# Delta attention with compact 32-token blocks and 32x32 tile products, given tile by tile

## The chip, the cores and the metric

One core of one Trainium2 chip runs the whole program in one launch. The metric is the device time of an execution in microseconds. The kernel computes four transformer layers in nine stages, one after the other with a barrier between them; the change touches the second stage, `delta_attention`, alone.

## The reference, cut to what matters

The stage computes layer 0's attention, for 2 sequences of 1024 tokens and 16 heads of 128 keys and 128 values. For each head and token a key `k`, a query `q`, a value `v`, a vector of decays `exp(g)` and a scalar `beta` come from projections and a short convolution; then

```python
def step(S, inp):
    q_t, k_t, v_t, g_t, b_t = inp
    S = S * jnp.exp(g_t)[..., None]
    kv = jnp.einsum('bhk,bhkv->bhv', k_t, S)
    delta = (v_t - kv) * b_t[..., None]
    S = S + k_t[..., None] * delta[..., None, :]
    o_t = jnp.einsum('bhk,bhkv->bhv', q_t * scale, S)
    return (S, o_t)
```

All numbers are fp32.

## The kernel before, in words

**Units and slots.** The work is cut into `NU0` = 64 units, each one head and one group of 512 tokens (`GRP`), that is four chunks (`NC`) of 128 tokens (`P`). A loop over slots `g` on each engine issues a fixed order of pieces; a unit starts every `SL` = 7 slots, and each piece of it has its slot (`K_AT`, `VT_AT`, ..., `LV_AT` = 17, `CHUNK_AT` = 24, `Y_AT` = 31), so the pieces of about five units lie beside each other in one slot. Every engine works its list in order; semaphores tie them, and a wait stops everything behind it on that engine. The order on each engine is written by hand, in the blocks `pe` (line 287), `act` (486), `pool` (597) and `dve` (674). Weights come by DMA per head on the SP queue (line 284).

**Levels.** Within a chunk the recurrence is unrolled into a triangular system. Its matrix, and the matrix from keys to outputs, are built in seven levels `lv` = 0 to 6 of doubling block size `h` = 2^lv, one level per slot. `products` (294) multiplies keys `kF` with the odd half-blocks of scaled keys and queries `kq`: per chunk one matmul with 128 columns of weights and 128 moving columns into the bank `lpd`. `mask` (689) on VectorE copies those entries that belong to the level (`pairs`) into `MA[:, lv]` (the system) and `MA[:, LV + u % 2]` (the output matrix). `scale` (606) on GpSimd multiplies the decays of the level into `kq` and `kF`. The first level's transpose is taken on TensorE (464).

**The inverse.** `Tm` holds the transposed inverse of the system built so far and `TT` the inverse, each 512 columns wide, a full 128x128 block per chunk. Each level from 1 to 6 updates them: X = `MA` times the even half-blocks of `Tm` (389), copied to `Xs` by ScalarE (555); Y = `TT` times X (434; 436 at level 6), subtracted from `Tm` by VectorE (829; 769 at level 6); `transposed` (302) turns `Tm` and ScalarE copies the odd half-blocks into `TT` (517). All this shares the bank `xy`.

**The chunks.** With the inverse, a unit's four chunks go one per slot through the state `St`: W = `kq` times `St` (372), `R` on VectorE (759), delta = `TT` times `R` (408), copied to `Dl` (552), then the state's update (449), and the outputs from the state (445) and from `MA`'s output matrix (450). Line 366 computes the diagonal of the output matrix, multiplied by the identity on VectorE (825). `VT`, `STAT`, `Z`, `KH`, `SUMS`, `OUT`, `Y` and `GATE` are the unit's other pieces: transposes of values, norms, decays, keys, the normalised and gated output and its projection (401).

**Array tiles.** A matmul may name a part of the 128x128 array by `tile_position` (first row, first column). Before the change only line 331 does so in this stage (weights of 32 columns); the last attention stage has 64-row and 64-column ones (1925, 1939, 1944). Line 436 has weights of 64 columns. An fp32 matmul appears in the trace as two MATMUL records and two LDWEIGHTS records, a transpose as one of each.

## Time and profile before

| what | value |
|---|---|
| median of 2 runs | 6401.66 us (6400.4 to 6402.93) |
| the profiled execution's own time | 6396.97 us |
| its span | 6394.8 us, 99261 instructions |
| TensorE busy | 5965.5 us, 93% |
| VectorE busy | 3804.0 us, 59% |
| ScalarE busy | 2694.1 us, 42% |
| GpSimd busy | 2288.9 us, 36% |

PE is TensorE's matmuls, PEld its weight loads, which run beside them; DVE is VectorE, ACT ScalarE, POOL GpSimd, SP the engine that issues DMAs. A busy share averages over nine stages with different limits, so the stage's own stretch is what counts. In a group's row, "128*64 128x64" is the used part of the array (rows*columns of weights) and the moving operand; after the bar stand busy time, the mean length of one record, and the engine's idle time just before the group with what ended it. Matmuls are pipelined: a record lasts longer than the step from one start to the next.

### The profile page before, as it was taken

What the parts mean: (1) busy time and instruction counts of PE and PEld (TensorE: products, weight loads), DVE (VectorE), ACT (ScalarE), POOL (GpSimd) and SP (SyncE); (2) the same over time, 40 slices, a digit from 0 to 9 for tenths busy, and PEclk for the clock granted to TensorE, in tenths of its full rate; (3) what the DMA queues carried; (4) which work ended last, traced back from release to release, by engine and by line L of the source; (5) the groups of instructions that cost most, each with busy time, mean ns of one, the idle gap of its engine ahead of it and who ended that gap; (6) DMA issues with size and microseconds to landing.
All of it is one profiled execution on the core that took longest, in us unless ns stands there. A gap on an engine that the chain in (4) does not pass through costs nothing. (4 is left out here: it accounts for less than half of the span.)

```text
span 6394.8 us, 99261 instructions
## 1 busy us (share of the span) xinstructions
PE 5965.5 (93%) x37522; PEld 4271.9 (67%) x37522; DVE 3804.0 (59%) x7226; ACT 2694.1 (42%) x5584; POOL 2288.9 (36%) x2602
## 2 busy tenths in 40 slices
PE   5999999999999999997999999989999999999999
PEld 3777777777777777775677777643335667766665
DVE  6778787787877878773344444266634444444322
ACT  4554555545555455541355555215662122222221
POOL 4677777777777777772000000020000011111100
PEclk8999999999999999998999999989999999999999
DMA  0000000000000000000000000000001011121200
GB/s 30 5 5 5 5 5 1 5 5 5 5 5 5 5 5 5 1 1 15 15 11 13 14 11 9 20 7 1 1 1 53 18 64 64 64 70 64 71 7 7
DMA packets 33926, 112.56 MB, mean 18 GB/s; under 512 B 4273, under 2 KB 9649, under 8 KB 33457
## 3 DMA queue, kind: packets, MB, share of 16 engines
q1 hardware_dynamic: 33456, 106.22, 4.9%
q8 instruction: 305, 5.00, 0.3%
q14 instruction: 165, 1.34, 0.1%
HBM read 104.11 MB, written 2.10 MB: 17 GB/s over the span
## 5 line engine op out<-in xcount | busy, mean ns | idle before, releaser
L616 POOL TENSOR_TENSOR d_kq<-d_kq,d_tot 128x512 f32<-128x512 f32 x448 | 543.0, 1212 | 742.2 <-PE d_lpd L299 731.3
L683 DVE SCALAR_TENSOR_TENSOR d_qkv<-d_raw,d_wts,d_qkv 128x512 f32<-128x512 f32 x576 | 531.9, 924 | 43.1 <-ACT d_qkv L492 35.6
L299 PE MATMUL d_lpd<-d_kq,d_kF 128*128 128x128 f32 x3584 | 520.5, 290 | 33.9 <-POOL d_kq L646 27.2
L299 PEld LDWEIGHTS d_lpd<-d_kq,d_kF 128*128 128x128 f32 x3584 | 458.9, 199 | 58.0 <-POOL d_kq L646 26.7
L389 PEld LDWEIGHTS d_xy<-d_Tm,d_MA 128*128 128x128 f32 x3072 | 388.6, 196 | 92.3 <-issue 90.8
L389 PE MATMUL d_xy<-d_Tm,d_MA 128*128 128x64 f32 x3072 | 406.1, 276 | 43.9 <-ACT d_TT L517 43.9
L694 DVE COPY_PREDICATED d_MA<-d_pairs,d_lpd 128x512 f32<-128x512 int32 x384 | 317.6, 827 | 134.2 <-PE d_lpd L299 123.4
L1001 POOL TENSOR_TENSOR f1rstd<-f1var,mhalf 128x4 f32<-128x4 f32 x4 | 4.0, 1009 | 1090.1 <-DVE f1var L1026 1090.1
L1787 DVE TENSOR_REDUCE r_nm<-r_ps 128x2 f32<-128x1024 f32 x256 | 307.8, 1222 | 142.4 <-PE r_ps L1606 142.3
L290 PE MATMUL d_fr<-xnT,d_wts 128*128 128x512 f32 x768 | 367.1, 601 | 5.3 <-DMA d_wts<-in_headw 5.3
L1885 PE MATMUL e_pj<-xnT,e_wts 128*128 128x512 f32 x768 | 348.1, 603 | 14.3 <-DMA e_wts<-in_w3all 12.3
L617 POOL TENSOR_TENSOR d_kF<-d_kF,d_tot 128x256 f32<-128x256 f32 x448 | 342.4, 764 | 0.0
L1707 ACT ACTIVATE r_pT<-r_ps 128x512 f32<-128x512 f32 x512 | 275.0, 598 | 148.5 <-PE r_ps L1614 147.9
L434 PE MATMUL d_xy<-d_Xs,d_TT 128*128 128x64 f32 x2560 | 329.5, 273 | 0.0
L697 DVE SCALAR_TENSOR_TENSOR d_lp<-d_lp,d_ez 128x512 f32<-128x512 f32 x448 | 310.9, 694 | 13.2
L434 PEld LDWEIGHTS d_xy<-d_Xs,d_TT 128*128 128x128 f32 x2560 | 318.6, 196 | 0.0
L1238 PEld LDWEIGHTS c_po<-c_pT,c_vt 128*128 128x128 f32 x2304 | 294.7, 191 | 20.8 <-ACT c_pT L1303 9.0
L1341 DVE TENSOR_TENSOR c_sc<-c_sc,c_mask 128x128 f32<-128x128 f32 x256 | 76.7, 300 | 382.5 <-PE c_sc L1193 382.3
L1238 PE MATMUL c_po<-c_pT,c_vt 128*128 128x128 f32 x2304 | 301.8, 276 | 0.2
L1606 PE MATMUL r_ps<-r_kT,r_qT 32*128 32x512 f32 x1024 | 294.1, 697 | 3.1 <-DVE r_nm L1787 1.6
L1193 PE MATMUL c_sc<-c_kT,c_qT 128*128 128x512 f32 (+3 forms) x768 | 290.2, 487 | 0.7 <-ACT c_qT L1264 0.7
L1614 PE MATMUL r_ps<-r_qT,r_kT 32*128 32x512 f32 x1024 | 279.5, 652 | 0.8 <-ACT r_pT L1707 0.8
...
## 6 DMA issues: line engine op xcount, KB each, us to landing
...
```

Of the source, the lines that this page charges most:

```text
L290: last = nc.tensor.matmul(fr[:, bank, :], w_of(u)[:, w0 + kd * P:w0 + (kd + 1) * P], T.xnT[:, kd, tok(u):tok(u) + GRP], start=(kd == 0), s ...
L299: last = nc.tensor.matmul(out[:, :, k], kF[:, u % 2, ch_(k)], moving[:, :, k, :, 1], start=True, stop=True)
L389: last = nc.tensor.matmul(mh(xy[:, j * 64:(j + 1) * 64], h), MA[:, lv, ch_(j)], even(Tm[:, ch_(j)], h), start=True, stop=True)
L434: last = nc.tensor.matmul(xy[:, 256 + j * 64:256 + (j + 1) * 64], TT[:, ul % 2, ch_(j)], Xs[:, j * 64:(j + 1) * 64], start=True, stop=True)
L616: nc.gpsimd.tensor_tensor(v, v, bc(bc(t_l[:, :, 0], 2, h), 1, 2), ALU.mult)
L617: nc.gpsimd.tensor_tensor(f, f, bc(t_l[:, :, 1], 2, h), ALU.mult)
L683: step = nc.vector.scalar_tensor_tensor(qkv[:, u % 3, x], raw[:, u % 2, x, i:i + GRP], tap(u, x, i), qkv[:, u % 3, x], ALU.mult, ALU.add)
L694: nc.vector.copy_predicated(into, bc(mh(pairs[:, lv], h), 1, 2), lpd[:].rearrange("p (x m h) -> p x m h", x=2, h=h)).then_inc(masked, 1)
L697: ch.link(nc.vector.scalar_tensor_tensor(lp[:], lp[:], LOG1P[i], ez[:], ALU.add, ALU.mult))
L1238: last = nc.tensor.matmul(po[:, 0:P], vt[:, n // (4 * QT) % 2, j], pT[:, n % 2, j * P:(j + 1) * P], start=(j == 0), stop=(j == t))
L1787: nc.vector.tensor_reduce(nm[:, t % 2, half, 4 * j + i0:4 * j + i0 + 2], ps[:, row_pair(row - 1):row_pair(row - 1) + 2], AX, ALU.max).then ...
L1885: last = nc.tensor.matmul(pj[:, x % 2, :], w[:, w0 + kd * P:w0 + (kd + 1) * P], T.xnT[:, kd, g * GRP:(g + 1) * GRP], start=(kd == 0), stop ...
```

## The change

The system is first built and inverted in compact blocks of 32 tokens: for levels 0 to 4 a matrix is kept as four bands of 32 partitions (`NB` = 4, `BW` = 32) with 32 columns for each chunk, 128 columns in all instead of 512 (`MB` for the masked products, `TB` for the inverse and its transpose). `products` below level `BL` = 5 gives, for each of four column tiles of the array, four chunks with 32 columns of weights and 32 moving columns. `in_blocks` gives 32x32 products, blocks outside and chunks inside. In levels 1 to 4 both Y and its transpose are computed as products (`Tb(0)`, `Xb` in either order), so that `transposed` and the copies into `TT` go. At level 5 ScalarE spreads the compact blocks into `TT` and `Tm` (six copies), at level 4 those of the output matrix into `MA` (four copies); level 5 works on pairs of blocks, level 6 on 64x64 tiles. A small identity `eye` is loaded besides. The wide products of levels 5 and 6, GpSimd's `scale`, the chunks and all other pieces are unchanged.

```diff
+BL = 5
+BW = 1 << BL
+NB = P // BW
...
-        MA = sb("MA", [P, LV + 2, GRP])
-        Tm, TT, Xs = sb("Tm", [P, GRP]), sb("TT", [P, 2, GRP]), sb("Xs", [P, GRP // 2])
+        MA, MB = sb("MA", [P, LV - BL + 2, GRP]), sb("MB", [P, BL + 2, P])
+        TB, TT, Tm = sb("TB", [P, 2, P]), sb("TT", [P, 2, GRP]), sb("Tm", [P, GRP // 2])
+        Xs = sb("Xs", [P, GRP // 2])
...
                 def products(u, lv):
                     h = 1 << lv
-                    out = lpd[:].rearrange("p (x c m h) -> p x c m h", x=2, c=NC, h=h)
-                    moving = kq[:, u % 2].rearrange("p x (c m two h) -> p x c m two h", c=NC, two=2, h=h)
-                    for k in range(NC):
-                        last = nc.tensor.matmul(out[:, :, k], kF[:, u % 2, ch_(k)], moving[:, :, k, :, 1], start=True, stop=True)
+                    if lv < BL:
+                        out = lpd[:, 0:P].rearrange("p (x c m h) -> p x c m h", x=2, c=NC, h=h)
+                        moving = kq[:, u % 2].rearrange("p x (c r m two h) -> p x c r m two h", c=NC, r=NB, two=2, h=h)
+                        for r in range(NB):
+                            for k in range(NC):
+                                last = nc.tensor.matmul(out[band(r), :, k], kF[:, u % 2, blk(k, r)], moving[:, :, k, r, :, 1], start=True, stop=True,
+                                                        tile_position=(0, BW * r), skip_group_check=True)
+                    else:
+                        out = lpd[:].rearrange("p (x c m h) -> p x c m h", x=2, c=NC, h=h)
+                        moving = kq[:, u % 2].rearrange("p x (c m two h) -> p x c m two h", c=NC, two=2, h=h)
+                        for k in range(NC):
+                            last = nc.tensor.matmul(out[:, :, k], kF[:, u % 2, ch_(k)], moving[:, :, k, :, 1], start=True, stop=True)
                     last.then_inc(p_mm, 1)
 
-                def transposed(u):
-                    for k in range(NC):
-                        last = nc.tensor.transpose(xy[:, ch_(k)], Tm[:, ch_(k)], T.ident[:])
-                    last.then_inc(tr_mm, 1)
+                def in_blocks(at_col, left, right, blocks, shift_in, shift_out):
+                    for r in blocks:
+                        for k in range(NC):
+                            i, o = band(r + shift_in), band(r + shift_out)
+                            last = nc.tensor.matmul(xy[o, at_col + k * BW:at_col + (k + 1) * BW], left(i, k, r), right(i, k, r), start=True, stop=True,
+                                                    tile_position=(i.start, o.start), skip_group_check=True)
+                    return last
+
+                Tb = lambda x: lambda i, k, r: TB[i, x, k * BW:(k + 1) * BW]
+                Xb = lambda i, k, r: Xs[i, k * BW:(k + 1) * BW]
+                eye_b = lambda i, k, r: eye[i, :]
+                low_b = lambda lv: lambda i, k, r: MB[i, lv, k * BW:(k + 1) * BW]
+                next_b = lambda i, k, r: MA[i, 0, blk(k, r + 1)]
...
-                        for j in range(NC):
-                            last = nc.tensor.matmul(fr[:, 2, ch_(j)], kF[:, u % 2, ch_(j)], qkv[:, u % 3, 0, ch_(j)], start=True, stop=True)
+                        for r in range(NB):
+                            for j in range(NC):
+                                last = nc.tensor.matmul(fr[band(r), 2, j * BW:(j + 1) * BW], kF[:, u % 2, blk(j, r)], qkv[:, u % 3, 0, blk(j, r)],
+                                                        start=True, stop=True, tile_position=(0, BW * r), skip_group_check=True)
...
+                        elif lv < 6:
+                            pe.wait_ge(tb_ready, 4 * ul + lv - 1)
                         else:
-                            pe.wait_ge(tm_ready, 5 * ul + lv - 1)
-                            pe.wait_ge(tt_ready, 5 * ul + lv - 1)
-                        h = 1 << lv
-                        for j in range(NC):
-                            last = nc.tensor.matmul(mh(xy[:, j * 64:(j + 1) * 64], h), MA[:, lv, ch_(j)], even(Tm[:, ch_(j)], h), start=True, stop=True)
+                            pe.wait_ge(t5_ready, ul + 1)
+                            pe.wait_ge(t_spread, ul + 1)
+                        if lv < 5:
+                            last = in_blocks(0, low_b(lv), Tb(1), range(NB), 0, 0)
+                        elif lv == 5:
+                            last = in_blocks(0, next_b, Tb(1), (0, 2), 0, 1)
+                        else:
+                            for j in range(NC):
+                                last = nc.tensor.matmul(xy[64:, j * 64:(j + 1) * 64], MA[0:64, 1, j * P + 64:(j + 1) * P], Tm[0:64, j * 64:(j + 1) * 64],
+                                                        start=True, stop=True, tile_position=(0, 64), skip_group_check=True)
...
                         pe.wait_ge(xs_ready, 6 * ul + lv)
-                        for j in range(NC):
-                            if lv < 6:
-                                last = nc.tensor.matmul(xy[:, 256 + j * 64:256 + (j + 1) * 64], TT[:, ul % 2, ch_(j)], Xs[:, j * 64:(j + 1) * 64], start=True, stop=True)
-                            else:
-                                last = nc.tensor.matmul(xy[0:64, 256 + j * 64:256 + (j + 1) * 64], Xs[:, j * 64:(j + 1) * 64], odd(TT[:, ul % 2, ch_(j)], 64)[:, 0],
-                                                        start=True, stop=True)
+                        if lv < 5:
+                            in_blocks(P, Xb, Tb(0), range(NB), 0, 0)
+                            last = in_blocks(2 * P, Tb(0), Xb, range(NB), 0, 0)
+                        elif lv == 5:
+                            in_blocks(P, Xb, Tb(0), (0, 2), 1, 0)
+                            last = in_blocks(2 * P, Tb(0), Xb, (0,), 1, 1)
+                        else:
+                            for j in range(NC):
+                                last = nc.tensor.matmul(xy[0:64, 256 + j * 64:256 + (j + 1) * 64], Xs[64:, j * 64:(j + 1) * 64],
...
-                        last = nc.tensor.matmul(co[:, ch_(k)], Dl[:, ch_(k)], MA[:, LV + uc % 2, ch_(k)], start=fresh, stop=True)
+                        if k == 0:
+                            pe.wait_ge(out_spread, uc + 1)
...
                         pe.wait_ge(mask0_ready, ul + 1)
-                        for j in range(NC):
-                            last = nc.tensor.transpose(xy[:, ch_(j)], MA[:, 0, ch_(j)], T.ident[:])
-                        last.then_inc(tr_mm, 1)
...
-                    if level and 1 <= lv < 6:
-                        pe.wait_ge(tm_ready, 5 * ul + lv)
-                        transposed(ul)
 
...
-                    if level and lv >= 2:
-                        act.wait_ge(tr_mm, 6 * ul + lv)
-                        h = 1 << lv - 1
-                        nc.scalar.activation(odd(TT[:, ul % 2], h), odd(xy[:], h), ACT.Copy).then_inc(tt_ready, 1)
+                    if level and lv == 5:
+                        act.wait_ge(tb_ready, 4 * ul + 4)
+                        for r in range(NB):
+                            nc.scalar.activation(TT[band(r), ul % 2].rearrange("p (c r i) -> p c r i", c=NC, r=NB)[:, :, r], c3(TB[band(r), 0]), ACT.Copy)
+                        for r in range(2):
+                            last = nc.scalar.activation(Tm[band(r)].rearrange("p (c r i) -> p c r i", c=NC, r=2)[:, :, r], c3(TB[band(r), 1]), ACT.Copy)
+                        last.then_inc(t_spread, 1)
+                    if level and lv == 4:
+                        act.wait_ge(masked, 7 * ul + 5)
+                        for r in range(NB):
+                            last = nc.scalar.activation(MA[band(r), 2 + ul % 2].rearrange("p (c r i) -> p c r i", c=NC, r=NB)[:, :, r], c3(MB[band(r), BL + ul % 2]), ACT.Copy)
+                        last.then_inc(out_spread, 1)
...
-                        nc.scalar.activation(Xs[:], xy[:, 0:256], ACT.Copy).then_inc(xs_ready, 1)
+                        rows, cols = (slice(64, P), 256) if lv == 6 else (slice(0, P), P)
+                        nc.scalar.activation(Xs[rows, 0:cols], xy[rows, 0:cols], ACT.Copy).then_inc(xs_ready, 1)
...
-                nc.gpsimd.memset(MA[:, 0:LV], 0.0).then_inc(consts_set, 1)
-                pool.wait_ge(consts_set, 4)
+                for t in (MA, MB, TT, Tm):
+                    nc.gpsimd.memset(t[:], 0.0).then_inc(consts_set, 1)
...
                 def mask(u, lv):
                     h = 1 << lv
-                    gap = LV + u % 2 - lv
-                    into = MA[:, lv:lv + gap + 1:gap].rearrange("p x (m two h) -> p x m two h", two=2, h=h)[:, :, :, 1]
+                    t, a, o, n = (MB, lv, BL, 64) if lv < BL else (MA, lv - BL, 2, 256)
+                    gap = o + u % 2 - a
+                    into = t[:, a:a + gap + 1:gap].rearrange("p x (m two h) -> p x m two h", two=2, h=h)[:, :, :, 1]
                     dve.wait_ge(p_mm, 7 * u + lv + 1)
-                    nc.vector.copy_predicated(into, bc(mh(pairs[:, lv], h), 1, 2), lpd[:].rearrange("p (x m h) -> p x m h", x=2, h=h)).then_inc(masked, 1)
+                    if lv == BL:
+                        dve.wait_ge(out_spread, u + 1)
+                    nc.vector.copy_predicated(into, bc(mh(level_pairs(lv), h), 1, 2), lpd[:, 0:2 * n].rearrange("p (x m h) -> p x m h", x=2, h=h)).then_inc(masked, 1)
 
...
-                        t = odd(TT[0:64, ul % 2], 64)
-                        nc.vector.tensor_tensor(t, t, mh(xy[0:64, 256:512], 64), ALU.subtract).then_inc(tt6_ready, 1)
+                        nc.vector.tensor_scalar(odd(TT[0:64, ul % 2], 64), mh(xy[0:64, 256:512], 64), -1.0, None, ALU.mult).then_inc(tt6_ready, 1)
...
+                        if ul:
+                            dve.wait_ge(t_spread, ul)
+                        nc.vector.tensor_tensor(c3(TB[:, 0]), bc(eye[:], 1, NC), c3(MB[:, 0]), ALU.subtract).then_inc(tt0_ready, 1)
...
-                        nc.vector.tensor_tensor(c3(Tm[:]), bc(T.ident[:], 1, NC), c3(xy[:]), ALU.subtract).then_inc(tm0_ready, 1)
+                        dve.wait_ge(tr_mm, ul + 1)
+                        nc.vector.tensor_tensor(c3(TB[:, 1]), bc(eye[:], 1, NC), c3(xy[:, 0:P]), ALU.subtract).then_inc(tm0_ready, 1)
...
                         dve.wait_ge(dg_mm, u + 1)
-                        nc.vector.tensor_tensor(c3(MA[:, LV + u % 2]), c3(fr[:, 2, :]), bc(T.ident[:], 1, NC), ALU.mult).then_inc(diag_ready, 1)
+                        if u >= 2:
+                            dve.wait_ge(out_spread, u - 1)
+                        nc.vector.tensor_tensor(c3(MB[:, BL + u % 2]), c3(fr[:, 2, 0:P]), bc(eye[:], 1, NC), ALU.mult).then_inc(diag_ready, 1)
                     if level and 1 <= lv < 6:
                         dve.wait_ge(yt_mm, 6 * ul + lv)
-                        h = 1 << lv
-                        nc.vector.tensor_tensor(even(Tm[:], h), even(Tm[:], h), mh(xy[:, 256:512], h), ALU.subtract).then_inc(tm_ready, 1)
+                        if lv < 5:
+                            nc.vector.tensor_tensor(TB[:], TB[:], xy[:, P:3 * P].rearrange("p (x i) -> p x i", x=2), ALU.subtract).then_inc(tb_ready, 1)
+                        else:
+                            for r in (0, 2):
+                                nc.vector.tensor_scalar(TT[band(r), ul % 2].rearrange("p (c r i) -> p c r i", c=NC, r=NB)[:, :, r + 1], c3(xy[band(r), P:2 * P]),
+                                                        -1.0, None, ALU.mult)
+                            nc.vector.tensor_scalar(Tm[band(1)].rearrange("p (c r i) -> p c r i", c=NC, r=2)[:, :, 0], c3(xy[band(1), 2 * P:3 * P]),
+                                                    -1.0, None, ALU.mult).then_inc(t5_ready, 1)
                     if chunk:
...
-    f["pairs"] = np.ascontiguousarray(np.stack([np.tile((j2 >> l) == 2 * (m2 >> l), (1, 4)) for l in range(LV)], 1).astype(np.int32))
+    low = [np.tile(((j2 % BW) >> l) == 2 * (m2[:, :BW // 2] >> l), (1, NC)) for l in range(BL)]
+    high = [np.tile((j2 >> l) == 2 * (m2 >> l), (1, NC)) for l in range(BL, LV)]
+    f["pairs"] = np.concatenate(low + high, 1).astype(np.int32)
```

## Rows read from the trace of the kernel before

**Rows 1.** The page, section 1: busy us (share of the span) x instructions.

```profile
PE 5965.5 (93%) x37522; PEld 4271.9 (67%) x37522; DVE 3804.0 (59%) x7226; ACT 2694.1 (42%) x5584; POOL 2288.9 (36%) x2602
```

**Rows 2.** Busy us by stretch: length, PE, PEld, DVE, ACT, POOL; clock, DMA, GB/s.

```profile
24.00:2940.00 2916.00, 2639.03 (x18415) 2125.31 (x18414) 2278.74 (x4441) 1454.69 (x2960) 2052.97 (x2382) 0.98 0.02 5
1504.00:1548.00 44.00, 40.95 (x294) 32.79 (x292) 35.12 (x70) 22.71 (x47) 32.04 (x37) 1.00 0.00 1
5361.12:5364.12 3.00, 3.00 (x49) 2.67 (x48) 2.31 (x4) 0.00 (x0) 0.00 (x0) 1.00 0.74 261
```

**Rows 3.** Line 346 alone: ns min/median/max, first and last start.

```profile
L346 PE MATMUL d_fr<-d_qkv,d_wsv x128: 592/595/1062, 53.0 to 2824.5; 128*128 128x512 f32 x128
```

**Rows 4.** TensorE's groups, 200 to 2600 us: busy, mean ns, idle before, releaser.

```profile
L299 PE MATMUL d_lpd<-d_kq,d_kF 128*128 128x128 f32 x3032 | 437.0, 288 | 20.1 <-POOL d_kq L646 18.1
L389 PE MATMUL d_xy<-d_Tm,d_MA 128*128 128x64 f32 x2600 | 340.7, 275 | 34.4 <-ACT d_TT L517 34.4
...
L304 PE MATMUL d_xy<-ident,d_Tm 128*128 128x128 f32 x1080 | 168.0, 278 | 9.7 <-DVE d_Tm L829 9.7
L401 PE MATMUL d_fr<-d_wo,d_og 128*128 128x256 f32 x432 | 107.7, 392 | 15.6 <-DVE d_MA L825 15.6
...
L408 PE MATMUL d_ca<-d_R,d_TT 128*128 128x128 f32 x434 | 96.0, 303 | 12.0 <-DVE d_R L759 11.9
L449 PE MATMUL d_ca<-d_Dl,d_khat 128*128 128x128 f32 x432 | 87.4, 284 | 66.1 <-ACT d_Dl L552 66.1
...
L372 PE MATMUL d_ca<-d_St,d_kq 128*128 128x128 f32 x382 | 82.9, 299 | 35.0 <-DVE d_St L835 21.7 <-DVE d_St L833 13.3
```

**Rows 5.** TensorE's timeline, around 1502 us: start us, us, instructions merged.

```profile
1502.11 1.00 PE L389 MATMUL d_xy<-d_Tm,d_MA 128*128 128x64 f32 x8
...
1503.23 1.06 PE L299 MATMUL d_lpd<-d_kq,d_kF 128*128 128x128 f32 x8
1504.12 1.02 PE L434 MATMUL d_xy<-d_Xs,d_TT 128*128 128x64 f32 x8
...
1505.70 0.61 PE L304 MATMUL d_xy<-ident,d_Tm 128*128 128x128 f32 x4
```

**Rows 6.** TensorE's timeline in the last attention stage, 5361 us.

```profile
5361.12 1.16 PE L1925 MATMUL e_md<-e_qkT 64*128 64x128 f32 x16
5362.22 1.09 PE L1939 MATMUL e_po<-e_at,e_v 128*64 128x128 f32 x16
5363.24 0.44 PE L1944 MATMUL e_po<-e_qdT,e_carry 64*64 64x128 f32 x4
5363.51 0.82 PE L1944 MATMUL e_po<-e_qdT,e_mid 64*64 64x128 f32 x12
5364.26 1.16 PE L1952 MATMUL e_md<-e_v,e_kvd 128*128 128x128 f32 x8
5365.26 0.69 PE L1885 MATMUL e_pj<-xnT,e_wts 128*128 128x512 f32 x1
```

**Rows 7.** Line 436's form, and narrow windows of the timeline (436, then 331).

```profile
L436 PE MATMUL d_xy<-d_TT,d_Xs x512: 222/222/366, 147.6 to 2933.8; 128*64 128x64 f32 x171
...
1522.71 0.40 PE L436 MATMUL d_xy<-d_TT,d_Xs 128*64 128x64 f32 x4
...
1499.12 0.64 PE L331 MATMUL d_fr<-d_sqs,d_pick 128*32 128x512 f32 x4
```

**Rows 8.** Copies and masks of VectorE and ScalarE, 200 to 2600 us.

```profile
L694 DVE COPY_PREDICATED d_MA<-d_pairs,d_lpd 128x512 f32<-128x512 int32 x326 | 270.1, 828 | 98.1 <-PE d_lpd L299 88.3
...
L517 ACT ACTIVATE d_TT<-d_xy 128x256 f32<-128x256 f32 x270 | 104.9, 389 | 149.9 <-PE d_xy L304 149.8
...
L552 ACT ACTIVATE d_Dl<-d_ca 128x128 f32<-128x128 f32 x217 | 60.9, 281 | 306.9 <-PE d_ca L408 306.9
```

**Rows 9.** Timeline of the stage's start, GpSimd and TensorE.

```profile
28.83 3.08 POOL L603 MEMSET d_MA<- 128x3584 f32 x1
...
32.46 8.06 PE L290 MATMUL d_fr<-xnT,d_wts 128*128 128x512 f32 x12 [5.34 <-DMA d_wts<-in_headw]
```

32 lines of the change are left out of this document (20 added, 12 removed).

## The prediction

> **What bounds the kernel now.** I read the page's busy shares first, then the busy time by stretch, then one projection's first and last start to get the rhythm, then the matmul groups with what they waited for, and the timeline last, to price one record. Of the span TensorE is busy 93% [rows 1]. The delta attention stage lasts from about 24 to 2940 us; inside it TensorE is busy 2639 of 2916 us, VectorE 2279, GpSimd 2053, ScalarE 1455 [rows 2]. Line 346 runs once per unit (one head and 512 tokens, 64 units): (2824.5 - 53.0) / 63 = 43.99 us per unit [rows 3]. In one such period TensorE works 40.95 us, VectorE 35.12, GpSimd 32.04, ScalarE 22.71 [rows 2]. So TensorE sets the pace, and what is left are waits: the seven groups of [rows 4] idle 192.9 us in 2400 us, or 54.6 units, 3.5 us per unit: 1.2 for `Dl` (L449), 0.64 for `St` (L372), 0.63 for the `TT` copy (L389), 0.37 for `kq` (L299), 0.29 for the diagonal (L401), 0.22 for `R` (L408), 0.18 for `Tm` (L304). VectorE and GpSimd have 9 and 12 us of air.
>
> **What one record costs.** An fp32 matmul leaves two records, each with its weight load; a transpose leaves one. Less the last one's own length, 0.288 us, eight products of L299 take (1.06 - 0.29) / 7 = 0.11 us a record [rows 4, 5]. L389 and L434 stream only 64 columns and cost the same (1.00 and 1.02 us for eight) [rows 5]: the 128 columns of weights set the step. A transpose takes (0.61 - 0.28) / 3 = 0.11 us. With 64 columns of weights the step is (0.40 - 0.222) / 3 = 0.059 us [rows 7]. Records on *different* tiles start together: four 512-column ones, 0.59 us each, lie within 0.64 us [rows 7], and sixteen on two tiles take 1.16 us where eight on the full array take 1.16 [rows 6].
>
> **The change, part by part, per unit.**
>
> *Counts.* Now the touched groups hold 56 (products) + 8 (diagonal) + 48 (X) + 48 (Y) + 24 (transposes) = 184 records, the rest 104, together 288; the trace has 294 in 44 us [rows 2]. After: nineteen sets of sixteen 32-wide matmuls (products of levels 0 to 4, the diagonal, four X, eight in four Y, the transposing one) are 608 records; level 5 has 16 + 24, level 6 has 8 + 8, the wide products of levels 5 and 6 have 16: 680, and 784 with the rest.
>
> *Array time.* The order is tile outside, chunk inside, so four successive matmuls share a tile and cannot lie on top of each other; only at three tile borders in a set can two start together. From 0.112 and 0.059 us at 128 and 64 columns, 53 ns per 64 columns, 32 columns give 0.032 us. No row shows 32 by 32; the bounds are 0.030 (half of 0.059) and 0.059 (nothing more to gain). I take 0.032, since the two rows lie on a line with their columns. A set costs 32 x 0.032 less the borders, 0.9 us, exactly what the wide group of eight costs (8 x 0.112). Now: 19 wide groups x 0.9 + 24 transposes x 0.11 + level 6's Y 0.46 = 20.2 us. After: 19 x 0.9 + level 5 0.5 + 0.7 + level 6 2 x 0.46 + two wide products 1.8 = 21.0 us. **+0.8 us.** A quarter of the area per matmul is paid back by four times as many of them.
>
> *Changing the array's shape.* From L1925 (64 rows) to L1939 (64 columns) and on to L1944 (64x64) and L1952 (full) the next group starts 0.20 us after the start of the last record before it (a group's end less the 0.27 to 0.29 us that a record lasts, [rows 4]), instead of 0.11 as from L1952 to L1885, where the shape stays [rows 6]. That is 0.09 us of draining, and then the first weights load uncovered: 0.03 us for 32 columns, 0.10 for 128. So 0.12 us into a narrow shape, 0.19 back. In program order of the new code the shape changes 33 times per unit (five times in each of the slots of levels 0, 1, 2, 3 and 6, four in those of 4 and 5), against 2 now (L436): 18 more into narrow shapes, 13 more into the full one: 18 x 0.12 + 13 x 0.19 = **+4.6 us.** Bounds: 0, if every drain falls into a wait, and 6 with 0.19 for all.
>
> *Waits removed.* The 20 transposes of `Tm` and the `TT` copies go, with 0.63 + 0.18 us of waits. More TensorE work stands between the first `St` and its use, and between scalings and products: of 0.64 + 0.37 + 0.22 us I take 1.1 as covered. `Dl` and the diagonal keep theirs. **-1.9 us** (bounds -2.0 and -0.8).
>
> *Waits added.* ScalarE gets four copies at level 4 and six at level 5, of 32 partitions x 128, for five `TT` copies of 0.389; the nearest row is 0.281 for 128x128 [rows 8]. Behind the level 4 copies stand the `stat` copy and `Xs`, behind those of level 5 `Xs`; the products between X and Y (0.9 us plus two shape changes) and the `stat` transposes cover most. **+0.3 us** (bounds 0 and 0.9: ten copies at 0.281 less five at 0.389, all exposed). VectorE's four masks shrink from 0.828 us [rows 8] and three of its 512-column subtractions too: priced at nothing, because it is not the bound; if TensorE's excess vanished that would count. `copy_predicated` of `out` at level 5 waits for a spread that was issued a slot earlier: nothing. GpSimd's scalings do not change. At the start its memsets grow from 3584 to 4224 columns, 3.08 to 3.6 us, ending near 32.5 us, while TensorE projects from 32.46 for 8 us before it needs them [rows 9]; the small identity's DMA lands in the same time.
>
> *Sum.* 0.8 + 4.6 - 1.9 + 0.3 = +3.8 us per unit, a period of 47.8; x 64 = +243 us. The profiled execution took 6396.97 us (span 6394.8), 5 us below the median of 6401.66, so 6640 either way.
>
> **Rivals.**
> *Tiles overlap in spite of the order* (faster). If loads and matmuls of the next tile passed those of the tile at work, four tiles would run at once, as L331's four do, and 648 narrow records would take a quarter: 15 us less. TensorE would fall to about 30 us and GpSimd's 32 and the level chain would bind; I put the period at 38: 6397 - 6 x 64 = 6010. It decides as soon as more than 4 us are overlapped. Against it: in L1925 to L1944 records start in pairs and never more, as the tiles alternate [rows 6]. The Trainium skill, TensorEngine Tiling (Array Packing), sections Theoretical Speedup and Key Properties, says that different tiles load and multiply in parallel and gives 4x for one dimension of 32; by that alone this rival would be the forecast. The rows grant it to neighbours in program order only. 0.12.
> *Drains are hidden* (no change): if changes of shape mostly fall where TensorE waits anyway, or the two narrow shapes need none, 1 to 2 us of the 4.6 remain: 6400 to 6530. For it: 3.5 us of waits; against: they sit at few places (L449, L372), the changes at all. 0.16.
> *Records have a floor.* If 32 columns still cost 0.059, 648 x 0.027 = +17.5 us: 6397 + 21.3 x 64 = 7760. The straight line through two rows speaks against. 0.12.
> *Supply.* The densest stretch is 49 records in 3.00 us, 0.061 each [rows 2]; if no more can be sustained, 784 x 0.061 = 47.8 plus the 1.2 us wait for `Dl`, 49.0: 6717. 0.10. The Trainium skill, TensorE: Matmul & The Clock Gate, section Wait — 56ns, not 53.3ns?, has about 62 ns per matmul for a sequencer that decodes in software; no run here shows in which mode this chip is, and by it the sum would be 784 x 0.062 + 1.2 = 49.8 us, about 6770.
>
> **Numbers.** The forecast (6530 to 6800) has 0.50. Likeliest time 6640. Two per cent, what a measurement of this kernel tells from no change, is 128 us: 6274 to 6530. Faster 0.12, same 0.15, slower 0.73. The range leaves out the faster rival and the full floor: 6440 (drains mostly hidden) to 7150 (a price of about 0.045 us, halfway between the bounds: 13 ns x 648 = 8.4 us more per unit, 6640 + 540).
>
> **What would show it.** Period of L346 near 47.8 us. A set of sixteen narrow matmuls spans 0.9 + 0.2 us from first start to last end: at 0.3 the overlap rival holds, at 1.7 the floor. Between groups of different shape the next start comes 0.20 us after the last. TensorE busy rises above 93%, VectorE's share falls, no wait for `TT` or `Tm` is left, and the `Dl` wait stays at about 1.2 us. I am wrong if the narrow records do not stand one behind another, or if waits for `Xs` or `TB` of over 1 us per unit appear on TensorE.

## Result: 2.96% slower, near the predicted time, by another route

The changed kernel takes 6587.59 us (median of two runs, 6582.71 to 6592.48) against 6401.66 before: a ratio of 1.0296, 95% interval 1.0277 to 1.0316. The forecast was 6640 within 6440 to 7150. The profiled execution of after spans 6590.7 us, 195.9 more than before's 6394.8, and all of it is in the delta attention stage: the projection that marks the unit (L346 before, L372 now) runs from 53.3 to 3016.6 us, a period of (3016.6 - 53.3) / 63 = **47.04 us** against 43.99 [rows 3], and 3.05 x 64 = 195 us.

The profile after, first its busy shares and TensorE's granted clock in 40 slices, then the clock row of before:

```profile
PE 6158.9 (93%) x69266; PEld 4298.0 (65%) x69266; DVE 3610.1 (55%) x7354; ACT 2755.4 (42%) x5904; POOL 2273.2 (34%) x2605
...
PEclk8898999899888989998899999999999999999999
...
PEclk8999999999999999998999999989999999999999
```

The share of TensorE is the same 93% as before [rows 1]. The stage is the first 19 slices, and of these 9 read 8 in the clock row; of before, 1 of the first 18 does. The stretches that answer to [rows 2], with one unit cut in four (us, then busy time of PE, PEld, DVE, ACT, POOL, then the clock):

```profile
24.00:3130.00 3106.00, 2826.17 (x50154) 2148.49 (x50152) 2085.69 (x4568) 1513.61 (x3277) 2035.97 (x2383) 0.90 0.02 6
1504.00:1551.00 47.00, 41.95 (x782) 32.60 (x782) 32.07 (x71) 23.64 (x51) 31.79 (x37) 0.93 0.01 3
1504.00:1526.00 22.00, 20.80 (x376) 15.79 (x374) 17.17 (x38) 10.65 (x26) 13.18 (x16) 1.00 0.01 2
1526.00:1533.00 7.00, 4.63 (x47) 3.76 (x45) 4.86 (x9) 1.84 (x5) 6.76 (x6) 0.78 0.01 4
1533.00:1541.00 8.00, 6.51 (x108) 4.70 (x107) 4.68 (x13) 4.62 (x8) 5.18 (x7) 0.76 0.01 3
1541.00:1551.00 10.00, 10.00 (x258) 8.35 (x260) 5.36 (x15) 6.53 (x14) 6.66 (x10) 1.00 0.01 3
```

The count of 782 records is the predicted 784. The clock was 0.98 in the stage before [rows 2] and is 0.90 now, and in this unit all of the loss lies between 1526 and 1541 us. TensorE's groups from 200 to 2600 us, to be read beside [rows 4]; that is 2400 / 47.04 = 51.0 units, where before has 54.6:

```profile
L299 PE MATMUL d_fr<-xnT,d_wts 128*128 128x512 f32 x600 | 341.8, 699 | 0.0
L310 PE MATMUL d_lpd<-d_kq,d_kF 128*32 128x32 f32 x8128 | 248.0, 206 | 71.8 <-POOL d_kq L692 70.4
L323 PE MATMUL d_xy<-d_TB,d_Xs 32*32 32x32 f32 x7264 | 217.7, 197 | 7.0 <-ACT d_Xs L600 6.9
...
L436 PE MATMUL d_fr<-d_wo,d_og 128*128 128x256 f32 x408 | 145.9, 521 | 9.7 <-DVE d_MB L877 9.7
...
L443 PE MATMUL d_ca<-d_R,d_TT 128*128 128x128 f32 x408 | 99.0, 326 | 2.6 <-DVE d_R L808 2.2
...
L488 PE MATMUL d_ca<-d_Dl,d_khat 128*128 128x128 f32 x406 | 83.7, 288 | 77.9 <-ACT d_Dl L596 77.9
...
L423 PE MATMUL d_xy<-d_Tm,d_MA 64*64 64x64 f32 x400 | 35.1, 231 | 16.6 <-DVE d_MA L743 16.6
```

The waits for `TT`, `Tm` and `St` are gone and that for `R` is 0.05 us per unit. But TensorE waits 71.8 / 51 = 1.41 us per unit for `kq0` (0.37 before), 1.53 for `Dl` (1.21) and 0.33 for the level 6 mask. And an untouched line has become slow: the Y projection, L436, takes 521 ns a record; the same work was 392 (L401 in [rows 4]).

**Where the period went.** For every pair of successive TensorE records of the same two lines I took the mean step from start to start in stretches at the full clock, and multiplied by how often the pair occurs. That is the unit's work at the full clock. What the same steps took beyond it I call clock cost; idle time is the rest. In us per unit, from the traces between 200 and 2600 us:

```
                          period  full-clock work  clock cost  waits
before                     43.99      39.87          0.58      3.52
after                      47.04      39.49          3.92      3.62
chunks outside             43.70      32.07          4.87      6.75
chunks outside + fill      43.05      34.78          3.32      4.95
after + fill at the waits  45.24      42.16          1.71      1.35
after + fill elsewhere     49.10      41.85          3.95      3.29
before + fill              44.98      41.72          0.47      2.79
before + six narrow        45.97      41.31          0.98      3.68
before + six wide          45.03      41.02          0.50      3.52
kq0 first                  50.58      42.46          4.95      3.15
kq0 first + fill           45.74      42.28          1.62      1.86
moved work, chunks outside 43.65      32.80          3.07      7.78
moved work + fill, same    44.99      34.41          2.77      7.80
before + moved work        44.84      39.00          1.55      4.28
```

(Some pairs never ran at the full clock, so their steps count as work: 8 us per unit in the row of kq0 first, 1.1 to 1.3 in the rows of moved work on the chunk order, 0.2 or less in the others. There the work is overstated and the clock cost is at least what stands in the row.) So the +3.05 us of the change are **-0.4 of work, +3.3 of clock, +0.1 of waits**. I had +5.4, 0 and -1.6. The traces' clock records add up to 68 us at the lower level (1.2 GHz) in these 2400 us before and 447 after. (Some expectations below carry such sums taken from a stretch 11 us earlier, up to 8 us larger.)

**Why kq0 is late.** GpSimd's timeline of the same unit:

```profile
1516.21 3.97 POOL L681 TENSOR_TENSOR d_pw<-d_st,d_half 128x20 f32<-128x20 f32 x1 [0.61 <-DVE d_sums L760]
...
1521.34 1.05 POOL L662 TENSOR_TENSOR d_kq<-d_kq,d_tot 128x512 f32<-128x512 f32 x1
...
1523.07 1.01 POOL L704 TENSOR_TENSOR d_rr<-d_ms,mhalf 128x4 f32<-128x4 f32 x1
...
1524.59 1.08 POOL L678 TENSOR_TENSOR d_hid<-d_pw,d_mlp 128x256 f32<-128x256 f32 x1
1525.64 1.05 POOL L685 TENSOR_TENSOR d_hid<-d_sums,d_mlp 128x256 f32<-128x256 f32 x1
1526.77 1.81 POOL L692 TENSOR_TENSOR d_kq<-d_qkv,d_tot 128x512 f32<-128x512 f32 x1
```

From the power of the sums to `kq0` it is one serial row of work, 10.6 us from 1516.21 to 1526.77, and it was as long before (10.7, 1511.87 to 1522.55). In the mean of the units between 200 and 2600 us the wait grows by 1.07 us. Counted from the `stat` transposes, TensorE arrives at the products of level 0 only 0.24 us earlier than before (13.79 us against 14.03), and `kq0` ends 1.0 us later, so that the products start 0.83 later. Of the 1.0, 0.59 is the start of the row (2.80 us after the `stat` transposes against 2.21): it needs the sums (L500, L459 before), and ahead of these now stand two sets of narrow products for Y instead of one wide group. The row itself is 0.21 longer, and `kq0` takes 1.68 us instead of 1.48. TensorE's timeline behind it:

```profile
1528.63 0.90 PE L310 MATMUL d_lpd<-d_kq,d_kF 128*32 128x32 f32 x32 [2.37 <-POOL d_kq L692]
1529.46 3.31 PE L436 MATMUL d_fr<-d_wo,d_og 128*128 128x256 f32 x8
...
1534.69 0.46 PE L488 MATMUL d_ca<-d_Dl,d_khat 128*128 128x128 f32 x2 [1.49 <-ACT d_Dl L596]
...
1537.04 2.08 PE L519 MATMUL d_fr<-d_g1T,d_wts 128*128 128x512 f32 x2
```

L436 takes 3.31 us; the same work took 1.99 at the full clock before (L401, at 1525.02 us). L519 takes 2.08, and took 1.02 (L480, at 1531.03). In this unit the clock falls behind the waits, at 1530.0 and 1536.8 us, and what pays is wide work that the change never touched. Over all units it is not so simple. Between 200 and 2600 us the clock falls 99 times. In the 14 us before 65 of these falls TensorE stood idle for 0.2 us or more in all, and they bring 283 us at the lower level. In those before the other 34 it did not, and they bring 164 us; these lie at one place of the unit, 18 to 24 us after the first record of L372, a stretch with narrow groups throughout. (The stretch of 14 us is my choice; 7 and 10 us give the same counts.) Before the change all 20 falls follow idle time. That the clock falls *because* of the waits was a guess here; the experiments below bear it out for the first kind.

### The profile page after: what moved, and what is told of

The parts are those of the page before. It is cut to its first block and busy times, and to the rows that moved or that the text cites. A ratio compares the mean times of both kernels' runs of the same rounds, so it can differ in the third digit from the quotient of the medians.

```text
span 6590.7 us, 163265 instructions
## 1 busy us (share of the span) xinstructions
PE 6158.9 (93%) x69266; PEld 4298.0 (65%) x69266; DVE 3610.1 (55%) x7354; ACT 2755.4 (42%) x5904; POOL 2273.2 (34%) x2605
## 5 line engine op out<-in xcount | busy, mean ns | idle before, releaser
L729 DVE SCALAR_TENSOR_TENSOR d_qkv<-d_raw,d_wts,d_qkv 128x512 f32<-128x512 f32 x576 | 551.8, 958 | 47.7 <-ACT d_qkv L528 45.1
L299 PE MATMUL d_fr<-xnT,d_wts 128*128 128x512 f32 x768 | 435.4, 697 | 5.4 <-DMA d_wts<-in_headw 5.4
L310 PE MATMUL d_lpd<-d_kq,d_kF 128*32 128x32 f32 x10240 | 313.7, 206 | 101.3 <-POOL d_kq L692 94.9
L310 PEld LDWEIGHTS d_lpd<-d_kq,d_kF 128*32 128x32 f32 x10240 | 276.6, 119 | 141.4 <-POOL d_kq L692 97.0
L596 ACT ACTIVATE d_Dl<-d_ca 128x128 f32<-128x128 f32 x256 | 72.1, 282 | 626.4 <-PE d_ca L443 626.3
L681 POOL TENSOR_TENSOR d_pw<-d_st,d_half 128x20 f32<-128x20 f32 x64 | 253.8, 3966 | 91.6 <-DVE d_sums L760 91.6
L323 PE MATMUL d_xy<-d_TB,d_Xs 32*32 32x32 f32 x9216 | 276.6, 197 | 9.3 <-ACT d_Xs L600 9.0
L527 ACT ACTIVATE d_raw<-d_fr 128x512 f32<-128x512 f32 x192 | 115.3, 600 | 363.8 <-PE d_fr L299 363.8
L323 PEld LDWEIGHTS d_xy<-d_TB,d_Xs 32*32 32x32 f32 x9216 | 240.2, 109 | 40.6 <-ACT d_Xs L600 20.3
```

Of the source, the lines that this page charges most:

```text
L299: last = nc.tensor.matmul(fr[:, bank, :], w_of(u)[:, w0 + kd * P:w0 + (kd + 1) * P], T.xnT[:, kd, tok(u):tok(u) + GRP], start=(kd == 0), s ...
L310: last = nc.tensor.matmul(out[band(r), :, k], kF[:, u % 2, blk(k, r)], moving[:, :, k, r, :, 1], start=True, stop=True, tile_position=(0, ...
L323: last = nc.tensor.matmul(xy[o, at_col + k * BW:at_col + (k + 1) * BW], left(i, k, r), right(i, k, r), start=True, stop=True, tile_positio ...
L729: step = nc.vector.scalar_tensor_tensor(qkv[:, u % 3, x], raw[:, u % 2, x, i:i + GRP], tap(u, x, i), qkv[:, u % 3, x], ALU.mult, ALU.add)
```

## The experiments

Each ratio is to the kernel before, measured beside the run (6395.5 to 6396.5 us), with 4 or 5 executions of the variant. "Than after" compares with the 6587.59 above, beside which before took 6401.66.

### 1. Chunks outside, tiles inside

```
-for r in range(NB):
-    for k in range(NC):
+for k in range(NC):
+    for r in range(NB):
         last = nc.tensor.matmul(out[band(r), :, k], ...
```

The same in `in_blocks` and in the diagonal's loop; the same instructions in another order.

> The changed kernel with chunks outside and tiles inside in every set of narrow matmuls (products below level 5, the diagonal, all 32x32 products), so that four neighbours in the order sit on four tiles. If neighbours on different tiles run together, a set of 32 records should shrink from about 0.7 us to about 0.3, TensorE's work by 19 x 0.4 = 7 us per unit. Theory (the new waits for kq and Dl and the low clock behind them set the time): most of it turns into waits on kq0 and on the level chain, the clock stays low, period about 45 us, 6450 us. Rival (TensorE's array time alone sets the pace): 7 us less per unit, 6588 - 450 = 6140 us.

Measured: 6374.39 us, ratio to before 0.9963 (0.9950 to 0.9976). Period 43.70. The windows row from 200 to 2600 us and some groups:

```profile
200.00:2600.00 2400.00, 2028.98 (x42869) 1408.57 (x42862) 1849.37 (x3895) 1286.64 (x2794) 1764.90 (x2028) 0.88 0.02 6
```

```profile
L436 PE MATMUL d_fr<-d_wo,d_og 128*128 128x256 f32 x432 | 177.9, 584 | 44.0 <-DVE d_MB L877 44.0
...
L310 PE MATMUL d_lpd<-d_kq,d_kF 128*32 128x32 f32 x8768 | 130.8, 202 | 76.7 <-POOL d_kq L692 73.5 <-POOL d_tot L664 0.8
...
L488 PE MATMUL d_ca<-d_Dl,d_khat 128*128 128x128 f32 x438 | 90.7, 290 | 82.7 <-ACT d_Dl L596 82.3 <-issue 0.4
...
L323 PE MATMUL d_xy<-d_TB,d_MA 32*32 32x32 f32 x864 | 27.5, 207 | 73.1 <-DVE d_TB L881 73.1
```

L310 is busy 130.8 us for 8768 records, where after's order needs 248.0 for 8128. 7.4 us per unit of work are gone, and only 3.3 arrive: 3.1 turn into waits (`TB` 73.1 / 54.9 = 1.3 us, `MB` 0.8, 0.6 before the products with `Xs`) and 1.0 more into clock (589 us at the lower level, clock 0.88). The work fell as expected (7), and the time lies between the two forecasts, 76 us under the theory's 6450 and 234 over the rival's 6140. That GpSimd's row and VectorE's level chain are in the way once TensorE has 32 us of work is read from the releasers in these rows.

### 2. kq0 at the head of GpSimd's slot

```
+if (u := at(g, KQ_AT)) is not None:
+    pool.wait_ge(w_ready, u + 1)
+    nc.gpsimd.tensor_tensor(kq[:, u % 2, 0], ...).then_inc(kq0_ready, 1)
 if (u := at(g, MLP_AT)) is not None:
...
 if level and 1 <= lv < 6:
     scale(ul, lv + 1)
-if (u := at(g, KQ_AT)) is not None:
...
```

> The changed kernel with one move on GpSimd: the product kq0 (L692) is issued at the head of its slot, ahead of the small pieces of the MLP (L677, L678, L685) and the scaling. Theory (the wait for kq0, 1.4 us per unit, and the fall of TensorE's clock behind it are what the change costs): the wait goes, the granted clock in the stage rises from 0.91 to about 0.97, together 3 to 4 us per unit: 6340 to 6400 us. Rival (the narrow matmuls themselves hold the clock down): only the wait goes, 1.4 x 64 = 90 us: 6500 us. Second rival (shape changes and narrow records are the cost, and another wait takes the place of this one): 6560 to 6600.

Measured: 6810.99 us, ratio 1.0649 (1.0633 to 1.0665): 223 us *slower* than after, period 50.58. Outside of every expectation. The wait for `kq0` is gone as intended:

```profile
L310 PE MATMUL d_lpd<-d_kq,d_kF 128*32 128x32 f32 x7488 | 253.5, 217 | 49.8 <-POOL d_tot L664 49.8
...
L488 PE MATMUL d_ca<-d_Dl,d_khat 128*128 128x128 f32 x376 | 87.7, 321 | 74.3 <-ACT d_Dl L596 74.3
```

and all waits together are less than after's (3.15 us per unit), but the clock is 0.80. One unit in stretches:

```profile
1504.00:1520.00 16.00, 15.99 (x312) 12.35 (x311) 10.07 (x23) 8.07 (x21) 6.10 (x7) 0.98 0.01 3
1520.00:1527.00 7.00, 7.00 (x71) 4.27 (x70) 5.65 (x15) 2.27 (x4) 5.30 (x7) 0.57 0.01 2
1527.00:1537.00 10.00, 7.62 (x95) 5.49 (x94) 7.95 (x14) 4.68 (x9) 9.39 (x9) 0.96 0.02 3
1537.00:1551.00 14.00, 13.44 (x193) 10.84 (x194) 5.93 (x18) 6.06 (x11) 9.11 (x13) 0.54 0.00 1
```

The long low stretch, 1537 to 1551, follows the waits for `Dl` (1.47 us) and `d_tot` (1.23), now close together. The short one, 1520 to 1527, follows 16 us in which TensorE was busy throughout, mostly with narrow groups. It is the rule and not a stray: of 94 falls 47 have no idle time of 0.2 us in the 14 us before them, and bring 321 of the 961 us at the lower level. So standing still is not the only thing ahead of a fall. This refutes my first wording of the theory.

### 3. Fill the two waits

```
+if ul:
+    pe.wait_ge(masked, 7 * ul)
+    for _ in range(2):
+        nc.tensor.matmul(lpd[:], wg1[:, 0], T.xnT[:, 0, 0:GRP], start=True, stop=True)
 pe.wait_ge(kq0_ready, ul + 1)
...
 if k == 0:
     pe.wait_ge(khat_ready, uc + 1)
+    nc.tensor.matmul(xy[:], wg1[:, 0], T.xnT[:, 0, 0:GRP], start=True, stop=True)
 pe.wait_ge(dl_ready, 4 * uc + k + 1)
```

Three extra 512-column matmuls per unit, whose results nobody reads.

> The changed kernel with useless work put in front of the two long waits of TensorE: two 512-column matmuls (1.72 us) before the wait for kq0 and one (0.86 us) before the first wait for Dl, 2.6 us of extra TensorE work per unit, into banks that are free there. The result's values don't change. Theory (the clock falls because TensorE stands still, and costs about 3 us per unit): the clock in the stage rises above 0.97 and the time falls in spite of the extra work, by 1.5 to 3 us per unit: 6400 to 6490 us. Rival (the low clock is incidental, TensorE's work sets the time): the extra work replaces waits of 2.9 us, no gain, 6590 to 6640 us.

Measured: 6473.02 us, ratio 1.0121 (1.0104 to 1.0138): with 2.7 us *more* work per unit it is 115 us faster than after. Against after the table has +2.7 of work, -2.2 of clock, -2.3 of waits. The lower level takes 195 us instead of 447, and of the wait for `kq0` 8.2 us are left in 53 units. The clock still falls 38 times, and none of these falls has 0.2 us of idle time in the 14 us before it: all falls behind waits are gone, and the other kind is left (34 falls and 164 us in after).

```profile
200.00:2600.00 2400.00, 2327.88 (x41663) 1716.55 (x41663) 1723.43 (x3757) 1244.84 (x2699) 1674.84 (x1958) 0.96 0.02 6
```

```profile
L310 PE MATMUL d_lpd<-d_kq,d_kF 128*32 128x32 f32 x8448 | 237.6, 198 | 12.5 <-POOL d_kq L695 8.2
...
L491 PE MATMUL d_ca<-d_Dl,d_khat 128*128 128x128 f32 x424 | 86.7, 286 | 30.6 <-ACT d_Dl L599 30.6
```

### 4 and 5. The price of changing the shape, on the kernel before

Six extra matmuls per unit, one before each X group from level 1 on, at the full array's shape or at 32x32:

```
 h = 1 << lv
+nc.tensor.matmul(xy[0:32, 0:32], MA[0:32, lv, 0:32], Tm[0:32, 0:32], start=True, stop=True,
+                 tile_position=(0, 0), skip_group_check=True)
 or
+nc.tensor.matmul(xy[:, 0:32], MA[:, lv, 0:P], Tm[:, 0:32], start=True, stop=True)
```

> The kernel before with one extra 32x32 matmul (two records) in front of each of the six X groups per unit, into a part of the bank that X then overwrites; the result's values don't change. It adds two shape changes each. At my price of 0.12 + 0.19 us and 2 x 0.03 for the records: 6 x 0.37 = 2.2 us per unit, 64 units, +142 us: 6544 us. If shape changes cost nothing: 6 x 0.06 = 0.4 us, +24 us: 6425 us.

> The kernel before with six extra matmuls of the full shape (128 rows and 128 columns of weights, 32 streamed columns) per unit, at the places where the run before it had six extra 32x32 ones. Nothing changes shape here. By my price of a record in the full shape, 0.112 us, twelve records cost 1.34 us per unit, +86 us: 6482 us. The 32x32 ones cost +129 us with less array time (12 x 0.032 = 0.38 us), so if the price of a change of shape is real this kernel is the faster of the two. Rival (what costs is any extra instruction with its semaphores and order, whatever its shape): 6525 us or more, as with the 32x32 ones.

Measured: narrow 6525.76 us, ratio 1.0200 (1.0185 to 1.0215), +129 us; wide 6463.93 us, ratio 1.0104 (1.0089 to 1.0119), +68 us. Three places of the narrow one's timeline, the third the next group:

```profile
1512.22 0.38 PE L372 MATMUL d_ca<-d_St,d_kq 128*128 128x128 f32 x2
1512.53 0.24 PE L388 MATMUL d_xy<-d_Tm,d_MA 32*32 32x32 f32 x2
1512.71 1.10 PE L390 MATMUL d_xy<-d_Tm,d_MA 128*128 128x64 f32 x8
```

The narrow matmul has a quarter of the columns and costs more, so the shape has a price. The narrow run came out near my sum (129 us against 142). By the table the work grows by 1.44 us, 0.24 per matmul, or 0.18 without its two records (2 x 0.032); the rest of the period's +1.98 is clock and waits. But 0.18 is a mean over unlike places and not the price of a pair of changes. In the timeline the last record of L372 starts at 1512.33, the narrow ones 0.205 and then 0.053 us later, L390 after 0.121 and its second record after 0.160, where the plain steps are 0.112, 0.032, 0.032 and 0.112: 0.093 + 0.021 + 0.089 + 0.048 = **0.25 us** for the pair. At four of the six places the steps are these; at the other two TensorE waits just before, and the first 0.09 is hidden. A wide record costs 1.15 / 12 = 0.096.

### 6. The same three fills, but not at the waits

```
+if 2 <= lv < 5:
+    nc.tensor.matmul(lpd[:], wg1[:, 0], T.xnT[:, 0, 0:GRP], start=True, stop=True)
 if lv < 5:
     last = in_blocks(0, low_b(lv), Tb(1), range(NB), 0, 0)
```

> The kernel after with three extra 512-column matmuls per unit (2.6 us of full-clock TensorE work, results overwritten), one each before the first narrow group of levels 2, 3 and 4, not before the two waits. Theory 1 (the clock falls because TensorE stands still before kq0 and Dl): nothing is gained back, 6588 + 64 x 2.6 = 6750 us, low-clock time as after. Theory 2 (the clock follows how full TensorE is over the whole neighbourhood, and narrow groups count for little): the low-clock time falls as it did with the fills at the waits, and the time is near 6473 plus what the fills hid there (1.9 us per unit), 6500 to 6600 us.

Measured: 6733.82 us, ratio 1.0531 (1.0514 to 1.0549). Theory 1 had 6750, theory 2 at most 6600. Waits hardly less, clock cost the same (3.95), 413 us at the lower level:

```profile
200.00:2600.00 2400.00, 2239.07 (x38111) 1642.58 (x38111) 1586.19 (x3457) 1141.83 (x2476) 1530.93 (x1802) 0.91 0.02 5
```

The same work brings 2.2 us of clock at the waits and nothing among the narrow groups: 49 falls behind idle time and 44 without are left.

### 7. Chunk order and fills together

> The kernel after with chunks outside and tiles inside, and the three extra 512-column matmuls before the first kq0 wait and the first Dl wait. Chunk order alone gave 6374 us with 597 of 2400 us at the half clock. Theory (that low clock is what ate the rest of its gain): the low-clock time falls to 200 us or less, the period from 43.7 to 42.0 to 42.8 us, 6266 to 6320 us. Rival (GpSimd's serial chain and the level chain set the period once the narrow groups overlap): 6374 us stays or the fills add up to 80 us.

Measured: 6331.61 us, ratio 0.9897 (0.9883 to 0.9912): **the fastest version found, 1.0% faster than before**, and 43 us faster than the chunk order alone, with more work. But above my band: the lower level still takes 399 us, not 200 or less. The `kq0` wait is gone and others have come up:

```profile
L445 PE MATMUL d_ca<-d_R,d_TT 128*128 128x128 f32 x444 | 103.3, 314 | 65.4 <-DVE d_R L811 58.8
...
L323 PE MATMUL d_xy<-d_TB,d_MA 32*32 32x32 f32 x880 | 26.4, 201 | 74.4 <-DVE d_TB L884 74.4
```

`R` 1.2 and `TB` 1.3 us per unit. VectorE's chain is what they wait for.

### 8. The control: fills on the kernel before

> The control for the fills: the kernel before with the same three extra 512-column matmuls at the same two waits. Before has a granted clock of 0.99 in the stage, so there is nothing to give back: 2.6 us per unit less what the waits for kq (0.37) and Dl (1.2) hide, +1.0 us, 6460 us (range 6440 to 6500). Rival (the fills help by something other than the clock, by keeping the queue or the order): no slower than 6400 us.

Measured: 6447.80 us, ratio 1.0081 (1.0066 to 1.0096): +52 us, period +0.99. Where the clock is 0.99 the fills only cost. Their gain on after is therefore nothing general.

### 9. kq0 first, with the fills

> The kernel after with kq0 at the head of GpSimd's slot (6811 us by itself, 962 of 2400 us at the half clock) and the three extra 512-column matmuls at the two waits. Theory (what the early kq0 lost, it lost by the clock, since TensorE's waiting only moved to other places): the fills bring the low-clock time under 500 us and the time to about 6500 us, 300 us faster with 2.6 us more work per unit. Rival (the loss is GpSimd's order: scale of level 0 and the tot products come later, and the unit waits for them): it stays at 6750 us or more.

Measured: 6514.75 us, ratio 1.0185 (1.0169 to 1.0201): 296 us faster than without the fills, 15 us beside the expectation. The lower level falls from 961 to 184 us:

```profile
200.00:2600.00 2400.00, 2303.23 (x41092) 1700.22 (x41092) 1719.71 (x3722) 1229.04 (x2667) 1650.91 (x1940) 0.96 0.02 6
```

What the early `kq0` lost, it lost by the clock. But it ends 42 us behind experiment 3, which leaves `kq0` where it was: GpSimd's other order gains nothing even so.

### 10 to 12. Real work in place of the fills

The Y projection goes behind the `Dl` product (and ScalarE's y copies behind its `Dl` copy), the V projection ahead of level 5's X:

```
+if (u := at(g, V_AT)) is not None:
...
+    project(u, 2, W_V, 1)
 if level and lv:
     pe.wait_ge(masked, 7 * ul + lv + 1)
...
 if chunk:
...
     nc.tensor.matmul(ca[:, 0:P], TT[:, uc % 2, ch_(k)], R[:, ch_(k)], start=True, stop=True).then_inc(dl_mm, 1)
+if (u := at(g, Y_AT)) is not None:
+    pe.wait_ge(diag_ready, min(u + 3, NU0))
...
```

> The kernel after with chunks outside and tiles inside, and with real work instead of fills at two of its waits: the Y projection (2 us) behind the Dl product instead of ahead of it, ScalarE's y copies behind its Dl copy, and the V projection (1.9 us) ahead of level 5's X instead of at the slot's end. Chunk order alone gave 6374 us, a period of 43.7 us, with 1.5 us of wait for Dl, 1.35 for TB and 597 of 2400 us at the half clock. Theory: both waits go and the low-clock time falls under 350 us, 41 to 42 us per unit, 6200 to 6290 us. Rival (the waits are set by the level chain and by GpSimd, and turn up at the next product): 6330 to 6380 us.

> The run before it with two extra 512-column matmuls before the kq0 wait (1.4 us there). If that wait still lets the clock fall, the fill (1.7 us) gives 0 to 100 us back: 6150 to 6250 us. If the moved work has already kept the clock up, the fill costs what the wait doesn't hide, up to 20 us, and a few tens of us more if GpSimd is by then the bound.

> The control for the moved work: the kernel before with the same three moves (Y projection behind the Dl product, y copies behind the Dl copy, V projection ahead of level 5's X). It has 1.2 us of wait for Dl per unit and a clock of 0.99, so the moves can be worth that wait and a part of the 0.63 us for the TT copy: 6300 to 6340 us. Rival (TensorE is 92% busy and the wait turns up at St or R): 6380 to 6400 us.

Measured: 6375.42 us (0.9965; 0.9952 to 0.9978), with fills 6444.05 (1.0071; 1.0054 to 1.0088), on before 6452.88 (1.0088; 1.0073 to 1.0104). All three forecasts are misses: the moves give nothing on the chunk order, where the rival's 6330 to 6380 holds, the fills on top cost 69 us and end far from 6150 to 6250, and the moves cost 56 us on before. The groups of the first show why:

```profile
L437 PE MATMUL d_ca<-d_R,d_TT 128*128 128x128 f32 x436 | 109.2, 333 | 140.3 <-DVE d_R L808 124.1 <-ACT d_R L544 9.9
...
L429 PE MATMUL d_xy<-d_Tm,d_MA 64*64 64x64 f32 x432 | 55.2, 301 | 190.6 <-DVE d_MA L743 190.6
```

The waits for `Dl` and `TB` are gone, as meant. In their place stand 190.6 / 55.0 = 3.5 us per unit for the level 6 mask and 2.6 for `R`, where experiment 1 had 0.1 and 0.5. By the order of the code the V projection at the slot's end had covered a part of the time that VectorE needs for that mask, and the Y block that for `R`; no run tests this by itself. I had asked which wait each block would cover, and not which one it already covered. Against experiment 1 the table has +1.0 of waits, +0.7 of work and -1.8 of clock, so more waiting went with a better clock here. The two fills hid nothing: +1.6 of work, the waits as they were, -0.3 of clock. On before the moves added 1.0 us of clock and 0.8 of waits and took 0.9 of work away; the waits there are now for `R`, `Tm` and GpSimd's `tot` and `kq0`, 0.5 to 1.1 us each.

## Why the prediction was right in the number and wrong in its terms

**What bounds the kernel**: right. TensorE set the pace before and sets it after.

**Array time, +0.8 us**: wrong in size and sign, about -3.7. The step that failed is "only at three tile borders in a set can two start together". Narrow windows of the timeline of after, each a longer piece of one set:

```profile
1505.49 0.31 PE L323 MATMUL d_xy<-d_TB,d_MB 32*32 32x32 f32 x4
...
1505.49 0.43 PE L323 MATMUL d_xy<-d_TB,d_MB 32*32 32x32 f32 x11
...
1505.49 0.89 PE L323 MATMUL d_xy<-d_TB,d_MB 32*32 32x32 f32 x32
```

A record lasts 0.19 us. The first four, on one tile, start over 0.31 - 0.19 = 0.12 us. The next seven start in the next 0.12: from the fifth record on the next tile runs beside the first. In the trace the steps on one tile are 0.032 us, exactly the predicted price, but each tile starts 0.153 us after the one before it, not 8 x 0.032 = 0.256, so three of eight records overlap at each border and not one. The mean step is (0.89 - 0.19) / 31 = 0.0226. Without a set's first step, 0.053 us, which belongs to the change of shape, the steps between 200 and 2600 us average 0.0212: a set costs 0.68 us instead of 0.9, and the 40 narrow records of level 5 cost 0.85 instead of 1.2. So 19 x 0.22 + 0.35 = 4.5 us too many stood in my sum.

**Changes of shape, +4.6 us**: right in kind and price, about 3.7 in all. Before the set above the last full record is followed after 0.205 us and the first narrow record after 0.053, where the same shape gives 0.112 and 0.032: 0.11 into a narrow shape, and I had 0.12. Behind it stands

```profile
1506.32 0.49 PE L443 MATMUL d_ca<-d_R,d_TT 128*128 128x128 f32 x2
```

The last narrow record starts at 1505.49 + 0.89 - 0.19 = 1506.19 and L443 0.12 us later, 0.09 more than the narrow step. Its second record follows after 0.49 - 0.275 = 0.21, which is 0.10 more than the plain step of 0.112: 0.19 back, exactly what I had. The median of such places in 2400 us is the same (0.205, 0.053, 0.121 and 0.213). Full groups with less to stream pay less for the second part (0.05 in experiment 4). I counted 33 changes, the trace has 32.2 per unit besides the two of L357. What the steps beside them take beyond the plain ones is 4.3 us per unit against 0.3 before. Of the difference, 0.3 stood at L408 and L445 before as well, whose second record came after 0.165 without a change; three changes fall into waits, which hide the first 0.09.

Together the two terms give 3.7 - 3.7 = 0. The table has -0.4. A record in front of a wait counts with its whole length of 0.275 us, not with its step, and there are 4.0 such places per unit instead of 6.2: that is -0.4.

**Waits removed, -1.9 us**: the named ones went (`TT` 0.63, `Tm` 0.18, `St` 0.64, `R` 0.17: 1.6). But I counted `kq` among those covered, and it grew by 1.0. I argued that more TensorE work stands before it. TensorE comes 0.24 us earlier instead, and `kq0` ends 1.0 later, 0.6 of it because the doubled Y products stand ahead of the sums on which GpSimd's row waits. Of GpSimd I had said only that its scalings do not change. **Waits added, +0.3**: `Dl`, the level 6 mask and `Xs` add 0.8. Together +0.1 instead of -1.6.

**The clock**: not in the sum at all, +3.3 us, the largest term of the result. Before, 3.5 us of waits per unit went with a clock of 0.99; I took the 0.98 to 1.00 of [rows 2] as a property of the stage. After has the same sum of waits, but they stand otherwise (in the unit shown 1.0, 2.4 and 1.5 us within 14 us), and two thirds of the low time, 283 of 447 us, follow such waits. The other third follows none and lies among the narrow groups.

So 5.8 us of work too many (4.5 in the sets, 0.9 in the changes of shape, 0.4 beside waits) stood against 3.3 of clock and 1.7 of waits too few, which leaves the 0.8 us by which the period of 47.8 was too long. The time was near by luck: errors of opposite sign cancelled. Of the signs I named, the set of sixteen (0.89 us, not 1.1), TensorE's share (93%, not more) and the `Dl` wait (1.53, not 1.2) did not hold.

**The rivals.** *Tiles overlap in spite of the order* (0.12) was half true: a border overlaps three records. I had let it decide from 4 us of overlap on; 4.5 were overlapped, and the clock and the new wait for `kq0` took them back. The Trainium skill, TensorEngine Tiling (Array Packing), section Key Properties, has different tiles multiply in parallel. With chunks outside the trace agrees; there one set reads

```profile
1523.79 0.45 PE L323 MATMUL d_xy<-d_TB,d_MB 32*32 32x32 f32 x32
```

which is (0.45 - 0.19) / 31 = 0.0084 us a record, a quarter of the 0.032 that one tile allows. In the order of the change the rule holds at the borders alone. *Floor* and *supply* (0.059 and 0.061 us a record, and the sum at 0.062) are refuted by the same numbers. *Drains are hidden*: refuted by the steps above and by experiments 4 and 5.

**What is shown and what is open.** Shown: the loss against before is clock (+3.3 of +3.05 us). Fills at the two waits give 2.2 us of it back (3) and leave no fall behind a wait; the same fills elsewhere don't (6), and where the clock is up they cost (8). So the greater part of the loss hangs on what TensorE does at those two places. A fill there both ends the idle time and adds wide work at that place; no run parts the two. Not shown: what sets off the falls without a wait, among the narrow groups. The same fills put into such groups (6) did not stop them. Nor does the sum of waits predict the clock: experiment 2 has less waiting than after and 4.9 us of clock cost or more per unit; experiment 10 waits 7.8 us per unit at a clock of 0.90 and experiment 1 6.8 us at 0.88.
